# Reordering one turn of a segmented attention loop, with part of its data held in bf16

## The reference

```
e     = leaky_relu(alpha_s[src] + alpha_d[dst], 0.2)   # layer 3 also times the edge's weight
m     = segment_max(e, dst);  ex = exp(e - m[dst])
s     = segment_sum(ex, dst)
out   = segment_sum(h[src] * ex / s[dst], dst)
```

## Time and profile before

| what | us |
|---|---|
| median of 3 runs (lowest, highest) | 6926.55 (6923.47, 6949.25) |
| the profiled execution, its own time | 6916.7 |
| its span, first to last instruction | 6914.9 |
| PE, DVE, ACT, POOL busy | 4848.1, 5023.9, 3845.9, 4869.6 |
| mean granted clock of PE, as a share of 2.4 GHz | 0.808 |
| first gather of 0a, of 0b, of 3 | 821.8, 1986.7, 5809.6 |
| last gather of 0a, of 0b, of 3 | 1836.0, 2999.9, 6830.4 |

### The profile page before, as it was taken

The page is one execution under the profiler, slowest core; times in us unless marked ns, Lnnn a source line. Parts: engine busy times, 40 slices in busy tenths (PEclk is TensorE's granted clock), DMA queues, the critical chain, the costliest instruction groups (busy, mean ns, idle before and its releaser), DMA issues. The chain is left out here.

```text
span 6914.9 us, 124558 instructions
## 1 busy us (share of the span) xinstructions
PE 4848.1 (70%) x21021; PEld 3523.0 (51%) x21022; DVE 5023.9 (73%) x11704; ACT 3845.9 (56%) x9024; POOL 4869.6 (70%) x4954
## 2 busy tenths in 40 slices
PE   6563277777647777775777777769999974777775
PEld 5452155555435555554555555546667653455553
DVE  6665377777757777787888888875555556777777
ACT  2341277677637676753444444426777763666664
POOL 0576677777477777757778878757777765777773
PEclk9655578788868888788989998979999985877777
DMA  5222255555335555525666666624444433555553
GB/s 166 66 70 53 80 135 137 135 137 135 92 92 136 136 135 137 134 77 147 187 178 187 181 187 179 184 72 130 129 130 130 130 102 103 136 135 135 135 134 91
DMA packets 596188, 894.68 MB, mean 129 GB/s; under 512 B 322611, under 2 KB 372960, under 8 KB 595700
## 3 DMA queue, kind: packets, MB, share of 16 engines
q0 software_dynamic: 245984, 649.30, 34.4%
q1 hardware_dynamic: 349700, 218.85, 11.9%
q10 hardware_dynamic: 416, 25.60, 1.1%
HBM read 859.36 MB, written 59.47 MB: 133 GB/s over the span
## 5 line engine op out<-in xcount | busy, mean ns | idle before, releaser
L1501 POOL DMA_INDIRECT at_ring<-tab_s,at_idx x808 | 776.0, 960 | 277.3 <-issue 204.7
L2391 POOL DMA_INDIRECT ae_ring<-tab_a,ae_idx x808 | 772.5, 956 | 256.0 <-issue 228.1
L1501 POOL DMA_INDIRECT at_ring_0a<-tab_s,at_idx_0a x808 | 767.5, 950 | 256.3 <-issue 206.9
L2001 POOL DMA_INDIRECT ad_ring<-tab_qv,ad_idx x808 | 772.9, 957 | 248.7 <-issue 208.0
L1501 POOL DMA_INDIRECT at_ring_0b<-tab_s,at_idx_0b x808 | 767.2, 950 | 255.4 <-issue 210.0
L1677 PE MATMUL at_po<-at_rows,at_hot 128*128 128x260 f32 x1616 | 557.6, 504 | 141.1 <-DVE at_begin L104 83.4
L1677 PE MATMUL at_po_0a<-at_rows_0a,at_hot_0a 128*128 128x264 f32 x1616 | 554.5, 500 | 139.6 <-DVE at_begin_0a L104 80.3
L1677 PE MATMUL at_po_0b<-at_rows_0b,at_hot_0b 128*128 128x264 f32 x1616 | 552.3, 499 | 138.9 <-DVE at_begin_0b L104 93.9
L2206 PE MATMUL ad_pk<-node_a,ad_hr 128*128 x1616 | 457.1, 432 | 223.3 <-DVE ad_prod L2076 122.1
L2285 ACT ACTIVATE ad_hot<-iota_row,ad_nrel 128x128 f32<-128x128 f32 x808 | 256.5, 388 | 462.0 <-PE ad_po L2225 462.0
L1677 PEld LDWEIGHTS at_po<-at_rows,at_hot 128*128 128x128 f32 x1616 | 384.2, 250 | 239.3 <-DVE at_begin L104 112.2
(11 more groups left out here) (521 smaller groups left out, 12537.1 us busy)
## 6 DMA issues: line engine op xcount, KB each, us to landing
at_rr_0a<-relrow_d SPq DMA_DIRECT2D x102, 256.0 KB
at_rr_0b<-relrow_d SPq DMA_DIRECT2D x102, 256.0 KB
ad_rr<-relrow_d SPq DMA_DIRECT2D x102, 256.0 KB
at_rr<-relrow_s SPq DMA_DIRECT2D x102, 256.0 KB
ae_feat<-attr_pad SPq DMA_DIRECT2D x808, 32.0 KB
rnk_lrow<-lorow_f SPq DMA_DIRECT2D x98, 256.0 KB
attr_pad<-in_edge_attr_dram ACTq DMA_DIRECT2D x1, 25000.0 KB, 81.8
at_ring_0a<-tab_s,at_idx_0a POOLq DMA_INDIRECT x808
```

What stands on the lines that cost most here:

```text
L1501: eng.indirect_dma_start(out=ring[:, t.slot * STEP + u, :], out_offset=None, in_=table, in_offset=bass.IndirectOffsetOnAxis(ap=idx[:, t.sl ...
L2001: eng.indirect_dma_start(out=ring[:, t.slot * STEP + u, :], out_offset=None, in_=table, in_offset=bass.IndirectOffsetOnAxis(ap=idx[:, t.sl ...
L2391: eng.indirect_dma_start(out=ring[:, k, :], out_offset=None, in_=table, in_offset=bass.IndirectOffsetOnAxis(ap=idx[:, k:k + 1], axis=0))\
```

## The change

- ACT: `ext0` moves from the head of the next turn to the tail of this one. `away0`, `hot0` and `parts` move ahead of `exp`. `own` and `selfs` move ahead of `alphas`; `picked` comes after it.
- PE: `spread1` moves from behind `back_turned` to just behind `trip4`, ahead of `mm12` to `mm15`. `joined` moves ahead of `back_turned`.
- `parts` is held in bf16, and the identity that it is multiplied with too (`ident16` takes the place of the unused tile `earlier`), so `joined` is three instructions. Its result moves to the PSUM tile of `scores`.
- DVE's and POOL's orders stay.

```diff
-        A = (["ext0", "away1", "hot1", "ext1", "away2", "hot2", "ext2", "far_r0", "hot_r0", "away3", "hot3", "ext3", "far_r1", "hot_r1", "exp", "alphas",
-              "away0", "hot0", "parts", "picked", "own"] + (["selfs"] if own_max else []))
+        A = (["away1", "hot1", "ext1", "away2", "hot2", "ext2", "far_r0", "hot_r0", "away3", "hot3", "ext3", "far_r1", "hot_r1",
+              "away0", "hot0", "parts", "exp", "own"] + (["selfs"] if own_max else []) + ["alphas", "picked", "ext0"])
         M = ["scores", "mm0", "mm1", "mm2", "mm3", "trip1", "mm4", "mm5", "mm6", "mm7", "trip2", "mm8", "mm9", "mm10", "mm11",
-             "trip3", "spread0", "trip4", "mm12", "mm13", "mm14", "mm15", "back_turned", "spread1", "joined"]
+             "trip3", "spread0", "trip4", "spread1", "mm12", "mm13", "mm14", "mm15", "joined", "back_turned"]
...
-            parts = sb(f"at_parts_{tag}", [P, 3, C, STEP], F32, c)
+            parts = sb(f"at_parts_{tag}", [P, 3, C, STEP], BF16, c)
...
-            ta = ps(f"at_ta_{tag}", [R, P], c)
+            ta = ps(f"at_ta_{tag}", [P, 2 * P], c)
...
-            joined = tt[:, 0:P]
+            scores_in, joined = ta[0:R, 0:P], ta[:, P:2 * P]
...
                         trip(4, "back", col4, line(run_b[:, :, :]), 1)
+                        spread(1, gs)
                         reduce(3)
+                        if spreads:
+                            eng.wait_ge(act, s.at("parts", t))
+                            for k in range(3):
+                                mm = eng.matmul(joined[0:C * STEP, :], parts[:, k, :, :].rearrange("p c u -> p (c u)"),
+                                                ident16[:, :], start=(k == 0), stop=(k == 2))
+                            m.did("joined", mm)
...
```

More of the change, by code:

```diff
@@ L110, in gnn_kernel @@
     ident = sb("ident", [P, P])
+    ident16 = sb("ident16", [P, P], BF16)
     iota_row = sb("iota_row", [P, P])
@@ L206, in _ @@
                                 st.own(eng, eng.tensor_scalar(minus_col[:, :], iota_col[:, :], -1.0, None, ALU.mult))
-                                for tile_, op in ((ident, ALU.is_equal), (earlier, ALU.is_lt), (later, ALU.is_gt)):
+                                for tile_, op in ((ident, ALU.is_equal), (ident16, ALU.is_equal), (later, ALU.is_gt)):
                                     st.own(eng, eng.tensor_scalar(tile_[:, :], iota_row[:, :], iota_col[:, :], None, op))
@@ L1706, in step @@
                             eng.sem_inc(told, 1)
-                            m.did("scores", eng.transpose(ta[:, :], picked[:, :, :].rearrange("p h u -> p (h u)"), ident[:, :]))
+                            m.did("scores", eng.transpose(scores_in, picked[:, :, :].rearrange("p h u -> p (h u)"), ident[:, :]))
                         else:
@@ L1722, in step @@
                         trip(4, "back", col4, line(run_b[:, :, :]), 1)
+                        spread(1, gs)
                         reduce(3)
+                        if spreads:
[4 more added lines that the diff above has]
+                            m.did("joined", mm)
+                        else:
+                            m.skip("joined")
                         if scores:
@@ L1733, in step @@
                             m.skip("back_turned")
[L1734 to L1742, removed]
                     run(eng, step)
@@ L1770, in extras @@
                                 return s.skip(f"ext{q}")
-                            eng.wait_ge(mat, free)
+                            if free is not None:
+                                eng.wait_ge(mat, free)
                             s.did(f"ext{q}", eng.activation(
@@ L1787, in step @@
                         if sums:
-                            done("alphas", a)
-                            extras(0, m.at("mm11", a))
                             one_hot(1, a, m.at("mm15", a))
@@ L1794, in step @@
                         else:
-                            s.skip("ext0", "away1", "hot1", "ext1", "away2", "hot2", "ext2")
+                            s.skip("away1", "hot1", "ext1", "away2", "hot2", "ext2")
                         hot_rows(0)
@@ L1803, in step @@
                         if scores:
[L1804 to L1808, removed]
                             eng.wait_ge(nrel_in[t.slot], t.lap * 16 + 16)
@@ L1811, in step @@
                         else:
-                            s.skip("exp", "alphas", "away0", "hot0")
+                            s.skip("away0", "hot0")
                         if spreads:
@@ L1816, in step @@
                                                           pb[:, :, :, :].rearrange("p u k c -> p k c u"), ACT.Copy))
+                        else:
+                            s.skip("parts")
+                        if scores:
+                            eng.wait_ge(vec, v.at("shrink", t))
+                            s.did("exp", eng.activation(expd[:, :], less[:, :], ACT.Exp))
+                        else:
+                            s.skip("exp")
+                        if spreads:
+                            eng.wait_ge(mat, m.at("joined", t))
+                            s.did("own", eng.activation(logits[:, 0, :], joined[0:R, :], ACT.Copy))
+                            if own_max:
+                                s.did("selfs", eng.activation(logits[:, 2, :], joined[R:2 * R, :], ACT.Copy))
+                        else:
+                            s.skip("own", *(["selfs"] if own_max else []))
+                        if scores:
+                            eng.wait_ge(mat, m.at("back_turned", t))
+                            s.did("alphas", eng.activation(al[:, :, :, :].rearrange("p k h u -> p (k h u)"), pe[:, 0:KX * R],
+                                                           ACT.Copy))
+                        else:
+                            s.skip("alphas")
+                        if spreads:
                             n = t.plus(1)
@@ L1824, in step @@
                                 .rearrange("p u h -> p h u"), ACT.Copy))
[L1825 to L1828, removed]
-                        else:
-                            s.skip("parts", "picked", "own", *(["selfs"] if own_max else []))
+                        else:
+                            s.skip("picked")
+                        if scores:
+                            done("alphas", t)
+                            extras(0, m.at("mm11", t) if sums else None)
+                        else:
+                            s.skip("ext0")
                     run(eng, step)
```

5 lines of the change are left out of this document (2 added, 3 removed).

## The result

The changed kernel takes 7413.2 us (median of 4, 7401.55 to 7429.8) against 6925.0 for the kernel before, run beside it: ratio 1.0705 with a 95% interval of 1.0686 to 1.0723. The forecast was 7015 and the range ended at 7110, so the result lies above every case that the prediction named. The profiled execution has a span of 7399.4 us, 484.5 more than before, and a mean granted clock of 0.747 (before 0.808).

A forecast was written before the change was run, and what follows sets the result against it. The prediction took one dependency chain through each compute turn as the bound, with no engine full. It added 52 us for 0a and 0b and 46 for layer 3 to 6916.7, giving 7014.7, taken as 7015; range 6895 to 7110.

The forecast's parts named there:

- `mm0` at 1.4: PE, turn start: `mm0` waits for `rows0` alone, starting near 1.4 us instead of 3.14; 0.95 us goes ahead of `rows2`.
- `exp` no longer on the chain: ACT, `away0`, `hot0`, `parts` ahead of `exp`: cost 0, `exp` done by 16.8 us while `back_turned` waits for PE's order.
- 0.35 for three bf16 instructions: PE, `joined` ahead of `back_turned`: three bf16 instructions in 0.35 us, bounds 0.2 and 1.0, before six in 1.35.
- rival B: Kinder clock gate: no slow stretch on the chain, lap 61.84 us in 0a and 0b, time 6922 us; chance 0.22.
- D: Shorter PE tail: `spread1` hides in the queue (0.3), `joined` costs 0.2, POOL's 20.1 us decides; 6873 us, chance 0.13.
- The sum leaves the half-clock stretches where they are.: PE's clock: the main forecast, chance 0.45, keeps the slow stretches of the earlier trace unchanged.
- The lap forecast: Three turns in 0a and 0b: `alphas` later by 0.52, 0.32 and 0.71 us, a lap +1.55 us.
- the 1.15 that I took: Third turn, `rows2` to `shrink`: DVE takes 8.19 us instead of 7.04 because `mm8` to `mm11` run at half clock.
- The signs that I gave for being wrong: Trace after: PE idle ahead of `mm12` or `back_turned`, or a lap at 60.3 us, POOL's pace.
- Rival C: Worse clock gate: `mm8` to `mm11` (or `mm12` to `mm15`) slow every turn, 21.76 us a turn, 7109 us; chance 0.18.
- one turn in three: Clock-gate rule on thin bursts: the trace before agreed only for this share of turns, with `mm8` to `mm11` slow.
- +26, +26 and +46: Added us for 0a, 0b and layer 3; in layer 3 `spread1` and `joined` were added in full, a lap +2.9 us.

## Why the prediction was wrong

**The order and its times were right, within some 0.3 us a turn.** `mm0` at 1.4 (measured 1.44); `exp` no longer on the chain; `back_turned` directly behind `joined`, and 0.35 for three bf16 instructions (0.33 at full clock). In the turns of 0b with no slow group of the changed kernel with 11 idle matmuls, `mm12` runs from 16.13 to 18.17 and `alphas` ends at 19.25 (medians); the forecast had 15.83, 17.87 and 19.0. `spread1` takes 1.05 and not 0.89, with a wait of 0.19 ahead of `trip4`. The all-fast lap of rival B was 61.84; with 20 idle matmuls and clock 1.00 it is 62.33. `spread1` does not hide, so D was rightly small. POOL did idle more, but as a follower.

**The failed step is "The sum leaves the half-clock stretches where they are."** The lap forecast was 61.44 + 1.55 = 63.0, with `alphas` ending at 19.0, 19.0 and 20.15. In the lap shown it ends at 20.76, 22.14 and 23.96: 1.76 + 3.14 + 3.81 = 8.71 more, which is 71.70 less 62.99. By place:

- `mm12` to `mm15` at 3.57, 3.73 and 3.88 instead of 2.04: 1.53 + 1.69 + 1.84 = 5.06.
- `rows2` at 9.41, 10.59 and 10.72 instead of 9.28, in the two late ones because `mm4` to `mm7` took 3.89: 2.88.
- The rest, 0.77: from `rows2` to `mm12` each turn takes 0.15 to 0.29 more than forecast (in the third the slow `mm8` to `mm11` cost more than the 1.15 that I took, and `spread1` more than 0.89), and in the third turn `joined` and `back_turned` ran at the lower clock too.

The signs that I gave for being wrong (PE idle ahead of `mm12` or of `back_turned`, a lap at 60.3) did not come: they watched the order and POOL, and none of them the clock.

**Rival C was the right mechanism at little more than a third of its price, and with the wrong place first.** It had one slow group in every turn (`mm8` to `mm11`, or `mm12` to `mm15` in brackets), 21.76, and a chance of 0.18. Measured in 0b are 1.7 more slow groups per turn and 23.87: +3.39 where C had +1.28. I carried the clock over as a property of the turn, when every PE edit of the change bore on it: 0.89 us of thin matmuls and waits put straight ahead of `mm12`, and a gap ahead of `mm4`. One row had shown the weak place: `mm12` to `mm15` of layer 3 at 3.83 us with `spread0` and `trip4` alone ahead of them, which in that trace is so in half of layer 3's turns. I used it as a price ("`alphas` waits for `mm15`") and did not ask what had slowed it. Instead I looked at the earlier trace rows and put the danger at `mm8`, which stayed as it was (0.31 of the turns, before 0.33) though `mm0` now starts at 1.44 in every turn.

The Trainium skill, page "TensorE: Matmul & The Clock Gate", section "HAM oscillation — how this bites in real kernels", which the prediction weighed, describes a loop of short bursts of matmuls with waits between them, whose clock falls back in every round. The trace after agrees in that each turn pays, with 3.02 slow groups a turn for 1.33. It does not show the page's reason, a wait for a DMA between the bursts: straight ahead of the slow `mm12` PE was busy for 2.30 of 2.60 us, at 1.00. The prediction held the rule to "one turn in three", the share before the change.

**By call:** forecast +26, +26 and +46; measured +162.8, +166.8 and +152.8. Layer 3, where I saw PE as slower to begin with, lost least: half of its turns had a slow `mm12` before.

**What is shown and what is not.** Shown: of the 488 us, 424 go when PE is kept at work in the same order (383 when the kernel before is given idle matmuls too); 404 go when `spread1` and `joined` stand behind `back_turned` again and `alphas` ahead of `parts`; `spread1` alone costs 4.8%, some 200 of its 329 us by the order, as estimated above (the changed kernel also has the early `mm0`, which the forecast credits with 0.95 us a turn); bf16 alone costs nothing. That the early `mm0` alone is harmless is not shown, as no run has it alone. Open: what in the change brings the clock down. The thin matmuls, the short waits between them (0.35 and 0.19 us in the turn shown) and the emptier gap between the turns all change together when `spread1` moves, and no run changes one of them alone. Filling that gap and the wait ahead of `mm8` (the 11 idle matmuls) left `mm12` to `mm15` slow in 47% of the turns of 0b. Open too is the part of the order: 33 us (64 - 31) against the kernel before, 74 (105 - 31) against it with idle matmuls. The forecast had 90 for it.

## What to carry to other kernels

A time of PE read from a trace holds at the clock of that stretch only. Before moving matmuls, list for each wide f32 group its clock and what PE did ahead of it; where the change puts thin matmuls or a gap there, carry as a main case that the group is slow in every turn (here 3.7 for 2.04). Then ask whether the group stands on the chain, for more slow groups cost nothing in the run with bf16 alone. Idle matmuls at the waits test this; put them at every wait at once, since the first 11 here gave back little over half, and treat the kernel before in the same way before you name what is left. Here they are also a small gain, 0.6% on the kernel before. A group that was never slow is not safe for that: in 0b `mm4` to `mm7` and `mm12` to `mm15` went from 0 to 0.71 and 1.00, while `mm8` to `mm11`, slow in a third of the turns, stayed.

## What the runs showed of the hardware

- The fall came late: the stretch of spreads ran at 1.00, busy 2.30 of 2.60 us, and the wide group behind it at 0.53. The clock of a stretch does not tell what the next one gets.
- Nine idle matmuls a turn raised the mean clock of the kernel before only from 0.808 to 0.849, and in 0b took the slow `mm0` (1.00 to 0.07 of the turns) for a slow `mm12` (none to 0.67). Fifteen, at two more places, left `mm12` never slow at a mean clock of 0.862. In these runs the place of the idle matmuls counts for more than the mean clock.
- More slow groups need not cost time: 2.00 a turn for 1.33 with bf16 alone, at 1.0006.
- The pattern repeats: four laps of the changed kernel in 0b one after another (from 2762.55 on) take between 71.67 and 71.70 us, each with two, three and four slow groups in its three turns.
- The same kernel took 6925 us in most runs and 9612 to 9697 in others, with single register instructions of DVE up to 1.4 us long in the latter.
